# Expert loop of a fused perceiver, attention and mixture-of-experts layer on one core: one product, the output base and the next rows move, a scale changes engine

## The chip, the cores and the metric

The kernel runs on one core of one Trainium2 chip. The metric is the device time of one launch in microseconds; weights are laid out by the host beforehand and are not part of it. The core has TensorE (PE, matmuls and transposes into PSUM), VectorE (DVE), ScalarE (ACT), GpSimd (POOL) and SyncE (SP), which here only issues transfers. Each engine works through its own instructions in order and meets the others at semaphores.

## The reference, cut to what matters

The input is 128 entries of 32 rows of 512 numbers, in float32. Three residual blocks follow one another: a cross-attention block over a context of 257 rows for each entry, 16-head self-attention, and a feed-forward layer that has a shared expert and a routed part for some rows:

```python
sh = _ln(silu(x1) * x2, s_ln_g, s_ln_b)               # shared expert, every row
shared_out = einsum('bth,dh->btd', sh, sw3) + sb3
x_moe = x[index_b, index_t]                            # the chosen rows
expert_scores = sigmoid(x_moe @ eg_w.T + eg_b)
top1_idx = argmax(expert_scores + exp_bias, axis=-1)
weights = softmax([shared_score, top1_score])
z = _ln(silu(h1) * h2, sel_ln_g, sel_ln_b)             # 8 experts, H = 256
out_all = einsum('meh,edh->med', z, ew3) + eb3
final_out = shared_out.at[index_b, index_t].set(shared_out[chosen] * shared_w + expert_out * expert_w)
```

With the given indices every chosen row that exists lies in one tile of 128 rows, so the routed part is computed for that tile alone.

## The kernel before, in words

The 4096 rows are cut into 32 tiles of 128 rows (four entries). Tile 31 is the first one of the tensor, worked last, and is the one that holds the chosen rows. Three slots of buffers hold three tiles that are at different stages at once. `run_pipeline` (L167 on) works in rounds: in round n each engine walks a list of pairs (lag, unit) and does unit `name` of tile n - lag, if it has not been done. The order of an engine's instructions is the order of its list and nothing else. There are three tables of such lists, written out by a planner: FIRST for rounds 0 to 3, ORDER for rounds 4 to 29 and LAST from round 30 to the end. A unit is one step of a tile: `turn_h2` is four PE transposes (or the ACT or POOL work on them), `hidden` the product with W1 (or DVE's layer norm behind it), `project_k_l` the low half of a product whose operand is split into two float16 parts, and so on. Such a product is `high`/`high_t` (L1638, L1661), which needs ACT's float16 copy (L738), and `low`/`low_t` (L1647, L1673), which needs ACT's float32 copy (L746) and POOL's remainder (L631). A layer norm is DVE's moments (L1105 to L1107), POOL's power (L622), and DVE's scaling (L1111, L1114, L1118).

The routed part has 8 experts, whose weights for two halves of four (12 MB in all) are loaded into the arena during rounds 32 and 33, when the products of the earlier stages no longer need it (`e_first` to `e_sixth` on SP). Experts 0 to 3 are worked inside the rounds of LAST, as units of tile 31: `e_moments`, `e_norm`, `e_turn` (normalised rows and their transpose `e_xn_t`), `e_logits` and `e_gate_a/b/c` (choice and weight), then for each expert k `e_in{k}` (eight float32 matmuls, L1785), `e_bias{k}` (DVE, L1408), `e_gate{k}` (ACT tanh, L855), `e_z{k}` (DVE, `z_made`, L1359), `e_zn{k}` (`z_normed`, L1368: offset L1370, scale by the row's weight L1371), `e_zt{k}` (two transposes and ACT's copy) and `e_out{k}` (four matmuls, L1808). `e_total` adds them up in `o`.

Experts 4 to 7, and any further chosen tile, are worked in a hardware loop behind the pipeline; `redo` holds the number of passes, which is 1 for these inputs: one pass, for the second half of tile 31. The loop's body on each engine: PE (L1848 on) does the first two products at once (`expert_in(0)`, `expert_in(1)`, L1853), the transpose of the coefficients (L1861) and the bias product (L1864), then for each z two transposes (L1870), the product after next, and the four matmuls into `ps_v` (L1879). DVE (L1460 on) makes the coefficients (L1476 to L1482), then `biased(0)` (L1472), and for each k `z_made` (L1362 to L1366) and `z_normed` (L1370, L1371), and `biased(k+1)`. Between the moments of z 0 and its norm it makes the output's base (L1492 to L1494) and behind it L1499; behind z 2 it normalises the rows of the next pass (L1503, L1505). After the last product it adds `ps_v` to `o` (L1508), and works the gate of the next pass (L1338 to L1357), the last instructions of the program. ACT (L890 on) copies the coefficients (L892), does the gates (L885), starts the load of the next x2 (L896), copies each turned z (L900), and for the next pass L905, L907, L909. POOL does the five powers (L663), SP loads the next `old` rows (L564) and stores `o` (L587). The work for the next pass is done in the last pass too, where nobody uses it.

`ps_a`, `ps_t`, `ps_v` and `ps_e` are PSUM banks; `last_slot` in a row can be any of the buffers of slot 2, which share one tensor.

## Time and profile before, and how to read it

| | us |
|---|---|
| three runs, median | 1475.81 (1474.77 to 1477.35) |
| profiled execution, its own time | 1476.32 |
| its span | 1474.5 |
| PE busy | 1371.7 (93%) |
| DVE busy | 1133.4 (77%) |
| ACT busy | 586.0 (40%) |
| POOL busy | 523.8 (36%) |
| granted TensorE clock, mean | 0.987 |

The span runs from the first to the last instruction; the profiled execution's own time is 1.8 us longer. A timeline row gives start, duration, engine, line, operation, output and inputs, count, and in brackets how long the engine had been idle before it and what ended that. Line numbers are those of the kernel before. A row of windows gives each engine's busy time in a stretch. The clock of 1.00 is 2.4 GHz, 0.50 is 1.2 GHz.

### The profile page before, as it was taken

What the parts mean: (1) busy time and instruction counts of PE and PEld (TensorE: products, weight loads), DVE (VectorE), ACT (ScalarE), POOL (GpSimd) and SP (SyncE); (2) the same over time, 40 slices, a digit from 0 to 9 for tenths busy, and PEclk for the clock granted to TensorE, in tenths of its full rate; (3) what the DMA queues carried; (4) which work ended last, traced back from release to release, by engine and by line L of the source; (5) the groups of instructions that cost most, each with busy time, mean ns of one, the idle gap of its engine ahead of it and who ended that gap; (6) DMA issues with size and microseconds to landing.
All of it is one profiled execution on the core that took longest, in us unless ns stands there. A gap on an engine that the chain in (4) does not pass through costs nothing.

```text
span 1474.5 us, 32944 instructions
## 1 busy us (share of the span) xinstructions
PE 1371.7 (93%) x13724; PEld 858.8 (58%) x13725; DVE 1133.4 (77%) x2349; ACT 586.0 (40%) x1108; POOL 523.8 (36%) x534
## 2 busy tenths in 40 slices
PE   7679999999999999999999999999999999998976
PEld 3355566656656666665666666666666666565533
DVE  5776678777788777877778787787777878777865
ACT  2543344444444444443444444444434444343221
POOL 0133334433434333343443433334334433333310
PEclk9899999999999999999999999999999999999989
DMA  9622444333333444433333344443333324435240
GB/s 349 250 95 107 144 144 144 135 105 116 134 105 128 143 144 144 144 139 108 114 136 106 119 144 144 144 143 141 118 108 131 120 104 144 144 137 222 81 164 22
DMA packets 38659, 201.38 MB, mean 137 GB/s; under 512 B 5096, under 2 KB 5992, under 8 KB 28400
## 3 DMA queue, kind: packets, MB, share of 16 engines
q1 hardware_dynamic: 37648, 198.93, 37.6%
q8 instruction: 108, 1.77, 0.5%
q10 hardware_dynamic: 864, 0.36, 0.1%
q14 instruction: 39, 0.32, 0.1%
HBM read 182.24 MB, written 17.04 MB: 135 GB/s over the span
## 4 chain that ended last, share of the span: by engine, by line
PE 67%; DVE 18%; issue 5%; POOL 4%; ACT 4%; DMA 1%; SPq 0%; DVEq 0%; POOLq 0%; ACTq 0%
PE ps_a L1638 10%; PE ps_a L1661 8%; PE ps_t L1661 8%; PE ps_t L1625 6%; PE ps_a L1647 6%; PE ps_a L1702 4%; PE ps_a L1673 4%; PE ps_v L1638 4%; PE ps_t L1638 3%; POOL rstd L622 3%; DVE stats L1105 3%; DVE arena L1236 3%; PE ps_t L1694 2%; PE ps_t L1673 2%; PE ps_t L1745 2%
## 5 line engine op out<-in xcount | busy, mean ns | idle before, releaser
L631 POOL TENSOR_TENSOR act_l<-act_t,act_h 128x512 f16<-128x512 f32 (+1 forms) x176 | 199.0, 1131 | 385.1 <-ACT act_t L746 222.8
L622 POOL TENSOR_TENSOR rstd<-var,mhalf 128x1 f32<-128x1 f32 x224 | 185.4, 828 | 301.8 <-DVE var L1107 301.2
L631 POOL TENSOR_TENSOR last_slot<-last_slot 128x512 f16<-128x512 f32 x80 | 89.5, 1118 | 168.3 <-ACT last_slot L746 97.4
L738 ACT ACTIVATE act_h<-ps_t,scale 128x512 f16<-128x512 f32 (+1 forms) x110 | 70.8, 644 | 156.3 <-PE ps_t L1625 156.3
L1661 PE MATMUL ps_a<-act_h,arena 128*128 128x128 f16 x1408 | 87.4, 221 | 18.0 <-ACT act_h L738 18.0
L1661 PEld LDWEIGHTS ps_a<-act_h,arena 128*128 128x128 f16 x1408 | 81.7, 99 | 28.3 <-ACT act_h L738 22.4
L1661 PE MATMUL ps_t<-act_h,arena 128*128 128x128 f16 x1408 | 88.0, 222 | 4.5 <-ACT act_h L738 4.5
L1661 PEld LDWEIGHTS ps_t<-act_h,arena 128*128 128x128 f16 x1408 | 82.4, 99 | 6.3 <-issue 2.9
L1638 PE MATMUL ps_a<-arena,act_h 128*128 128x512 f16 x352 | 83.4, 380 | 1.6 <-ACT act_h L738 1.6
L746 ACT ACTIVATE act_t<-ps_t,scale 128x512 f32<-128x512 f32 (+1 forms) x110 | 70.3, 639 | 34.8 <-PE ps_t L1625 34.8
L1236 DVE TENSOR_SCALAR arena<-ps_a,unscale 32x512 f32<-32x512 f32 x64 | 48.2, 754 | 43.7 <-PE ps_a L1673 42.5
L1105 DVE BATCH_NORM_STATS2 stats<-rows 128x6 f32<-128x512 f32 x110 | 76.4, 695 | 3.8
L1625 PE MATMUL ps_t<-ident,rows 128*128 128x128 f32 x352 | 55.4, 280 | 14.0 <-DVE rows L1111 8.9
L1638 PE MATMUL ps_a<-w_parts,act_h 128*128 128x512 f16 x264 | 65.0, 383 | 1.3 <-ACT act_h L738 1.3
L1118 DVE SCALAR_TENSOR_TENSOR rows<-rows,rstd,beta 128x512 f32<-128x512 f32 x66 | 49.4, 748 | 21.5 <-POOL rstd L622 21.5
L1718 PE MATMUL ps_a<-arena,p_t 128*32 128x512 f32 x512 | 63.1, 611 | 1.5 <-ACT p_t L793 1.5
L1276 DVE STREAM_TRANSPOSE arena<-rows 32x512 f32<-32x512 f32 x88 | 61.8, 702 | 2.8
L1625 PEld LDWEIGHTS ps_t<-ident,rows 128*128 128x128 f32 x352 | 40.2, 141 | 36.1 <-DVE rows L1111 22.5
L738 ACT ACTIVATE last_slot<-ps_t,scale 128x512 f16<-128x512 f32 (+1 forms) x50 | 32.2, 644 | 62.8 <-PE ps_t L1625 62.8
L1638 PEld LDWEIGHTS ps_a<-arena,act_h 128*128 128x128 f16 x352 | 32.0, 98 | 41.9 <-ACT act_h L738 9.4
L1114 DVE SCALAR_TENSOR_TENSOR rows<-rows,mv,gamma 128x512 f32<-128x512 f32 x66 | 49.6, 751 | 0.0
L1702 PE MATMUL ps_a<-arena,q_t 128*32 128x257 f32 x704 | 44.3, 394 | 4.6 <-ACT q_t L783 4.6
(358 smaller groups left out, 3086.2 us busy)
## 6 DMA issues: line engine op xcount, KB each, us to landing
arena<-in_ctx_t SPq DMA_DIRECT2D x32, 2056.0 KB, 8.4
arena<-in_ctx_n SPq DMA_DIRECT2D x32, 2048.0 KB
ctx_last<-in_ctx_last SPq DMA_DIRECT2D x32, 256.0 KB
arena<-in_ew SPq DMA_DIRECT2D x8, 1024.0 KB, 6.1
x_in<-in_x SPq DMA_DIRECT2D x22, 256.0 KB, 7.2
x_scratch<-rows SPq DMA_DIRECT2D x22, 256.0 KB, 8.7
out<-rows SPq DMA_DIRECT2D x22, 256.0 KB, 2.0
arena<-in_ew SPq DMA_DIRECT2D x8, 512.0 KB, 7.3
```

Source lines behind the costliest of these rows:

```text
L622: nc.gpsimd.tensor_tensor(rstd[s][:], var[s][:], mhalf[:], ALU.pow).then_inc(rstd_ready[s], 1)
L631: nc.gpsimd.tensor_tensor(act_l[s][:, chunks], act_t[s][:, chunks], act_h[s][:, chunks], ALU.subtract).then_inc(act_l_ready[s], 1)
L738: nc.scalar.activation(act_h[s][:, 0:width // P].rearrange("p c r -> p (c r)"), bank[s][:, 0:width], ACT.Copy, scale=scale[:, k:k + 1]).th ...
L746: nc.scalar.activation(act_t[s][:, 0:width // P].rearrange("p c r -> p (c r)"), bank[s][:, 0:width], ACT.Copy, scale=scale[:, k:k + 1]).th ...
L1105: chain(nc.vector.bn_stats(stats[s][:], rows))
L1236: nc.vector.tensor_scalar(kbd[rows, :, :, h, :], ps_a[s][rows, :].rearrange("p (c g k) -> p c g k", c=C, g=G), unscale[rows, K_WATTN:K_WAT ...
L1625: mm = nc.tensor.transpose(out[s][:, c * P:(c + 1) * P], rows[s][:, lo + c * P:lo + (c + 1) * P], ident[:])
L1638: nc.tensor.matmul(bank[s][:], act_h[s][:, c, :], w[:, part, c, lo:lo + D], start=(c == 0 and part == 0), stop=False, skip_group_check=True)
L1647: mm = nc.tensor.matmul(bank[s][:], act_l[s][:, c, :], w[:, 0, c, lo:lo + D], start=False, stop=(c == chunks - 1), skip_group_check=True)
L1661: nc.tensor.matmul(bank[s][:, m * P:(m + 1) * P], w[:, part, c, lo + m * P:lo + (m + 1) * P], act_h[s][:, c, :], start=(m == 0 and c == 0 ...
L1673: mm = nc.tensor.matmul(bank[s][:, m * P:(m + 1) * P], w[:, 0, c, lo + m * P:lo + (m + 1) * P], act_l[s][:, c, :], start=False, stop=(c == ...
L1702: mm = nc.tensor.matmul(ps_a[s][T * g:T * (g + 1), 0:S], q_t[s][:, c, T * g:T * (g + 1)], ctx_t[:, c, g, :], start=(c == 0), stop=(c == C ...
```

## The change

Four edits to the loop, and new LAST lists for all four engines.

1. `expert_in(0)` of a pass is issued at the end of the pass before; for the first pass it is a new pipeline unit `e_in4` of tile 31 in round 34, ahead of `turn_z`. It waits for e_u_ready and for the last part of the expert weights.
2. DVE does `biased(0)` ahead of the coefficients, ACT `gated(0)` ahead of the copy of them. PE does the transpose of the coefficients behind `expert_in(1)`, then `expert_in(2)`, then the bias product; `expert_in(3)` stands behind the transposes of z 0.
3. The rows of the next pass and the output's base go behind the last z. The next x2 and `old` are loaded into buffers of their own at the start of the pass (`x2_next`, `old_next`) and ACT copies both into place at its end.
4. The scale of z by the row's weight goes from DVE (L1371) to ACT, as an activation in place behind DVE's offset; each gate goes ahead of the copy of the turned z. In the pipeline's `e_zn{k}` the scale stays on DVE.

In LAST, PE's list has in its second half (from `project_out` to `project_q`, for the tiles of rounds 30 and 31) the order of ORDER again, but `turn_xn`, `project_self` stand side by side, `project_v` and `head_scores` have changed places, and `head_mix` stands ahead of `turn_p` and `value_self_l`. For tile 31 `e_turn`, `e_logits`, `e_in0` go ahead of `turn_w`, `e_in1` behind `project_out`, `e_in3` behind `project_v_l`, `e_out1` and `e_zt2`, `e_out2` behind `project_out_l`, `e_zt3` behind `turn_x2n` and `e_out3` behind `ffn_in_l`.

```diff
 LAST = {
-    "pe": [(2, "project_k_l"), (3, "ffn_out"), (3, "ffn_out_l"), (1, "turn_pc"), (2, "project_q_l"), (2, "e_zt1"),
...
-        (1, "e_out0"), (0, "project_query_l"), (0, "context_scores"), (2, "ffn_in"), (2, "ffn_in_l"),
-        (1, "turn_x1n"), (1, "project_k"), (1, "project_q"), (2, "turn_z")],
+    "pe": [(3, "e_in4"), (3, "turn_z"), (2, "project_k_l"), (1, "turn_pc"), (2, "project_q_l"), (3, "ffn_out"),
+        (1, "context_mix"), (3, "ffn_out_l"), (2, "project_v"), (2, "head_scores"), (2, "project_v_l"),
+        (1, "e_turn"), (0, "turn_xn"), (1, "e_logits"), (0, "project_self"), (1, "e_in0"), (2, "e_out1"),
+        (2, "e_zt2"), (0, "project_self_l"), (0, "value_self"), (1, "turn_w"), (0, "self_scores"),
+        (1, "context_out"), (1, "context_out_l"), (2, "e_in3"), (2, "head_mix"), (0, "turn_p"), (0, "value_self_l"),
+        (0, "self_mix"), (2, "project_out"), (1, "e_in1"), (1, "turn_h2"), (2, "project_out_l"), (1, "hidden"),
+        (1, "hidden_l"), (2, "e_out2"), (1, "e_zt0"), (1, "e_in2"), (0, "turn_h"), (2, "turn_x2n"), (2, "e_zt3"),
+        (0, "project_query"), (0, "project_query_l"), (2, "ffn_in"), (1, "e_out0"), (0, "context_scores"),
+        (2, "ffn_in_l"), (1, "turn_x1n"), (1, "project_k"), (2, "e_out3"), (1, "project_q"), (1, "e_zt1")],
...
 # SP, in the loop
-                    sp.wait_ge(e_x2_used, i + 1)
+                    sp.wait_ge(x2_copied, i + 1)
                     sp.sem_inc(stats_seen, 1)
                     load_old(i + 1)
+                    sp.wait_ge(e_old_loaded, 16 * i + 32)
...
 # ACT, in the loop
+                    gated(i, 0)
                     act.wait_ge(coef_turned, i + 1)
                     nc.scalar.copy(coef_t[:], ps_gate[0:NE, P:2 * P]).then_inc(coef_t_ready, 1)
-                    gated(i, 0)
...
                     for k in range(EH):
+                        act.wait_ge(z_normed, EH * i + k + 1)
+                        nc.scalar.activation(z, z, ACT.Copy, scale=mine_coef[:, k:k + 1]).then_inc(e_z_ready, 1)
+                        if k + 1 < EH:
+                            gated(i, k + 1)
                         act.wait_ge(e_z_turned, EH * (i + 1) + k + 1)
                         nc.scalar.copy(z_t.rearrange("p c r -> p (c r)"), ps_t[s_b][:, 0:H]).then_inc(e_z_t_ready, 1)
...
+                    act.wait_ge(xn_turned, i + 2)
+                    nc.scalar.copy(flat_rows(e_xn_t), ps_t[s_last][:]).then_inc(xn_t_ready, 1)
+                    act.wait_ge(e_x2_used, i + 1)
+                    nc.scalar.copy(x2[:], x2_next[:])
+                    act.wait_ge(e_old_loaded, 16 * i + 32)
+                    nc.scalar.copy(old[:], old_next[:]).then_inc(x2_copied, 1)
...
 # DVE, in the loop
+                    biased(0)
                     step(nc.vector.tensor_copy(now[:], flags[:, bass.ds(half * 2, 2)]))
...
-                    biased(0)
                     for k in range(EH):
                         dve.wait_ge(e_z_turned, EH * (i + 1) + k)
                         z_made(step, EH * (i + 1), k)
-                        if k == 0:
...
-                        z_normed(step, (1 + EH) * (i + 1) + k + 1 + (k > NEXT_ROWS), mine_coef[:, k:k + 1])
+                        dve.wait_ge(e_rstd_ready, (1 + EH) * (i + 1) + k + 1)
+                        nc.vector.scalar_tensor_tensor(z, z, e_rstd[:], sel_b, ALU.mult, ALU.add).then_inc(z_normed, 1)
                         if k + 1 < EH:
                             biased(k + 1)
...
+                    dve.wait_ge(e_x2_loaded, 16 * i + 32)
+                    expert_moments(step, x2_next[:])
+                    dve.wait_ge(e_rstd_ready, (1 + EH) * (i + 1) + EH + 1)
+                    nc.vector.tensor_scalar(e_xn[:], x2_next[:], e_mv[:, 0:1], e_rstd[:], ALU.subtract, ALU.mult
+                                            ).then_inc(xn_ready, 1)
+                    dve.wait_ge(x2_copied, i + 1)
+                    dve.sem_inc(stats_seen, 1)
+                    dve.wait_ge(e_out_stored, 16 * i + 16)
+                    step(nc.vector.tensor_scalar(o, o, now[:, 1:2], None, ALU.mult))
+                    step(nc.vector.scalar_tensor_tensor(o, old[:], now[:, 0:1], o, ALU.mult, ALU.add))
+                    step(nc.vector.tensor_tensor(old[:], old[:], x2[:], ALU.subtract))
+                    step(nc.vector.scalar_tensor_tensor(o, old[:], one[:, 7:8], o, ALU.mult, ALU.add))
+                    dve.sem_inc(e_x2_used, 1)
...
 # PE: the new unit, and the loop
+                def e_in_next(s, r, tile):
+                    if tile == FINAL:
+                        pe.wait_ge(e_u_ready, EH)
+                        pe.wait_ge(part_loaded[3], PART_COUNTS[3])
+                        for c in range(C):
+                            mm = nc.tensor.matmul(ps_a[s_a][:], e_xn_t[:, c, :],
+                                                  of_arena(HALF + EW12[0] + c * 2 * H, 2 * H), start=(c == 0),
+                                                  stop=(c == C - 1))
+                        mm.then_inc(e_u_done, 1)
...
-                    expert_in(0)
-                    expert_in(1)
+                    expert_in(1, half)
                     pe.wait_ge(coef_ready, i + 1)
                     nc.tensor.transpose(ps_gate[0:NE, P:2 * P], pick[:, 3, :], ident[:]).then_inc(coef_turned, 1)
+                    pe.wait_ge(e_u_ready, EH * (i + 1) + 1)
+                    expert_in(2, half)
                     pe.wait_ge(coef_t_ready, i + 1)
...
-                        if k + 2 < EH:
-                            pe.wait_ge(e_u_ready, EH * (i + 1) + k + 1)
-                            expert_in(k + 2)
-                        if k == EH - 1:
-                            gate_logits(i + 2)
+                        if k == 0:
+                            pe.wait_ge(e_u_ready, EH * (i + 1) + 2)
+                            expert_in(3, half)
...
+                    turn_expert_rows(ps_t[s_last], i + 2)
+                    gate_logits(i + 2)
+                    expert_in(0, half_next)
```

## Rows read from the trace of the kernel before

**Rows 1.** Windows by stage: a round of ORDER, rounds 30, 32, 33, the loop

```profile
core 0: us, PE busy (x) PEld busy (x) DVE busy (x) ACT busy (x) POOL busy (x), PEclk, DMA share, GB/s
1221.75:1262.60 40.85, 39.67 (x425) 25.45 (x423) 32.06 (x67) 16.96 (x34) 15.92 (x16) 1.00 0.36 128
1262.60:1305.90 43.30, 39.94 (x425) 25.63 (x422) 34.15 (x67) 16.92 (x33) 15.64 (x16) 1.00 0.37 135
...
1349.20:1398.10 48.90, 42.94 (x321) 24.10 (x319) 38.01 (x87) 14.80 (x30) 13.79 (x15) 0.97 0.45 164
1398.10:1434.00 35.90, 26.81 (x165) 12.06 (x162) 24.71 (x49) 9.07 (x18) 7.60 (x9) 0.92 0.43 162
1434.00:1474.50 40.50, 28.77 (x71) 12.93 (x71) 22.43 (x64) 4.01 (x12) 3.25 (x5) 0.88 0.08 26
```

**Rows 2.** Timeline of PE in round 30: its two longest waits

```profile
1288.58 1.90 PE L1638 MATMUL ps_a<-arena,last_slot 128*128 128x512 f16 x8 [0.78 <-ACT last_slot L738]
...
1296.07 1.94 PE L1702 MATMUL ps_a<-arena,q_t 128*32 128x257 f32 x32 [0.78 <-ACT q_t L783]
```

**Rows 3.** Timeline of tile 31 in round 33, up to the loop

```profile
1417.79 0.75 DVE L1282 SCALAR_TENSOR_TENSOR rows<-ps_a,unscale,rows 128x512 f32<-128x512 f32 x1 [0.30 <-PE ps_a L1647]
...
1420.34 0.55 DVE L1111 TENSOR_SCALAR rows<-rows,mv,rstd 128x512 f32<-128x512 f32 x1 [0.67 <-POOL rstd L622]
...
1425.33 0.75 DVE L1293 SCALAR_TENSOR_TENSOR rows<-ps_a,unscale,b 128x512 f32<-128x512 f32 x1 [4.44 <-PE ps_a L1647]
...
1429.39 0.69 PE L1625 MATMUL ps_t<-ident,v_n 128*128 128x128 f32 x2 [4.10 <-DVE v_n L1118]
...
1433.49 0.75 DVE L1316 SCALAR_TENSOR_TENSOR rows<-ps_a,unscale,b 128x512 f32<-128x512 f32 x1 [2.05 <-PE ps_a L1647]
```

**Rows 4.** Timeline of rounds 32 and 33: durations used in the sum

```profile
1356.54 0.72 ACT L757 ACTIVATE v_n<-v_n,row_scale 128x512 f32<-128x512 f32 x1 [0.42 <-DVE row_scale L1186]
...
1397.01 0.39 PE L1625 MATMUL ps_t<-ident,v_n 128*128 128x128 f32 x2
...
1399.90 0.75 DVE L1316 SCALAR_TENSOR_TENSOR rows<-ps_a,unscale,b 128x512 f32<-128x512 f32 x1
...
1402.43 3.70 PE L1785 MATMUL ps_a<-arena,last_slot 128*128 128x512 f32 x8
...
1418.44 1.98 PE L1808 MATMUL ps_t<-arena,p_t 128*128 128x512 f32 x4 [0.46 <-ACT p_t L862]
```

**Rows 5.** Windows of PE ahead of the loop: busy, granted clock, DMA

```profile
1424.00:1428.00 4.00, 1.29 (x6) 1.00 0.01 3
1428.00:1432.00 4.00, 2.05 (x6) 0.56 0.00 0
```

**Rows 6.** Timeline of the loop's first part on VectorE

```profile
1436.23 0.17 DVE L1476 COPY now<-flags 128x2 f32 x1 [1.27 <-issue]
...
1440.17 0.69 DVE L1472 TENSOR_TENSOR last_slot<-ps_a,arena 128x512 f32<-128x512 f32 x1 [2.79 <-PE ps_a L1853]
...
1447.62 0.69 DVE L1494 TENSOR_TENSOR last_slot<-last_slot 128x512 f32<-128x512 f32 x1
```

**Rows 7.** Timeline of the loop from z 1 to z 2

```profile
1452.78 0.43 DVE L1364 SCALAR_TENSOR_TENSOR p_n<-last_slot 128x256 f32<-128x256 f32 x1 [1.53 <-ACT last_slot L885]
...
1455.02 0.48 DVE L1370 SCALAR_TENSOR_TENSOR p_n<-p_n,rstd,ctx_last 128x256 f32<-128x256 f32 x1 [0.44 <-POOL rstd L663]
...
1455.54 0.35 DVE L1371 TENSOR_SCALAR p_n<-p_n,mine_coef 128x256 f32<-128x256 f32 x1
...
1456.68 0.42 DVE L1362 SCALAR_TENSOR_TENSOR last_slot<-last_slot 128x256 f32<-128x256 f32 x1 [0.18 <-PE ps_t L1870]
...
1456.95 0.42 ACT L885 ACTIVATE last_slot<-last_slot 128x256 f32<-128x256 f32 x1
```

**Rows 8.** Timeline of the loop's end on VectorE

```profile
1470.06 0.69 DVE L1508 TENSOR_TENSOR last_slot<-ps_v,last_slot 128x512 f32<-128x512 f32 x1 [3.15 <-PE ps_v L1879]
...
1473.88 0.16 DVE L1357 TENSOR_TENSOR one<-one,sel 128x1 f32<-128x1 f32 x1
```

More of the change, by code:

```diff
@@ L127 @@
 LAST = {
-    "pe": [(2, "project_k_l"), (3, "ffn_out"), (3, "ffn_out_l"), (1, "turn_pc"), (2, "project_q_l"), (2, "e_zt1"),
-        (1, "context_mix"), (2, "head_scores"), (2, "e_in3"), (0, "turn_xn"), (2, "project_v"), (2, "project_v_l"),
-        (1, "turn_w"), (2, "e_out1"), (0, "project_self"), (1, "e_turn"), (0, "project_self_l"), (1, "e_logits"),
-        (0, "value_self"), (1, "e_in0"), (0, "self_scores"), (2, "e_zt2"), (1, "context_out"), (1, "context_out_l"),
-        (0, "value_self_l"), (0, "turn_p"), (2, "head_mix"), (1, "e_in1"), (0, "self_mix"), (2, "e_out2"),
-        (2, "project_out"), (2, "project_out_l"), (1, "e_zt0"), (2, "e_zt3"), (2, "e_out3"), (1, "turn_h2"),
-        (1, "hidden"), (0, "turn_h"), (1, "hidden_l"), (1, "e_in2"), (0, "project_query"), (2, "turn_x2n"),
-        (1, "e_out0"), (0, "project_query_l"), (0, "context_scores"), (2, "ffn_in"), (2, "ffn_in_l"),
-        (1, "turn_x1n"), (1, "project_k"), (1, "project_q"), (2, "turn_z")],
@@ L156 @@
+    "pool": [(3, "turn_z"), (0, "xn_moments"), (0, "turn_xn"), (1, "e_norm"), (2, "e_zn2"), (2, "head_scores"),
+        (1, "turn_w"), (1, "context_out"), (2, "head_mix"), (1, "e_zn0"), (0, "self_mix"), (2, "e_zn3"),
+        (1, "turn_h2"), (2, "project_out"), (0, "turn_h"), (1, "hidden"), (2, "turn_x2n"), (1, "out_norm"),
+        (1, "e_zn1"), (1, "turn_x1n"), (2, "silu")],
 }
@@ L563, in load_old @@
                 def load_old(i):
[L564 removed]
+                    sp.dma_start(old_next[:], a["out"][bass.ds(tile_of(sp, i), 1)].rearrange("a p d -> (a p) d")
                                  ).then_inc(e_old_loaded, 16)
@@ L1839, in _ @@
                     **{f"e_in{k}": e_in(k) for k in range(EH)}, **{f"e_zt{k}": e_zt(k) for k in range(EH)},
-                    **{f"e_out{k}": e_out(k) for k in range(EH)}})
+                    **{f"e_out{k}": e_out(k) for k in range(EH)}, "e_in4": e_in_next})
                 pe.wait_ge(out_ready[s_b], r_b + 1)
```

83 lines of the change are left out of this document (29 added, 54 removed).

## The prediction

> **What bounds the kernel now.** I read the windows by stage first. In a round of ORDER, PE is busy 39.67 of 40.85 us; rounds 30 and 31 (one stands for both) do the same tile work in 43.30 with 39.94 busy, so their surplus is waiting [rows 1]. Round 32 is PE with gaps (42.94 of 48.90), round 33 and the loop are not PE's: 26.81 of 35.90 and 28.77 of 40.50 us [rows 1]. There the timeline shows a chain through DVE, with PE, ACT and POOL taking single steps between. Only what comes after 1262.6, some 212 us, can change: the tables of the rounds before 30 are untouched.
>
> In the loop DVE starts at 1436.23, and its first real work, the bias of product 0, comes at 1440.17 after 2.79 us of waiting for PE [rows 6], which started eight half-rate matmuls only when the pipeline was over. Then the first z waits for a gate that stands on ACT behind the coefficients, the base is made while z 0 is due, the gate of each z stands behind the copy of the z before, and the next rows stand between z 2 and z 3. The output is added at 1470.06 and the last instruction ends at 1474.04 [rows 8]. So the loop takes DVE 1474.04 - 1436.23 = 37.81 us, for four z whose steps are about 4 us each.
>
> **The loop after the change**, with DVE's first instruction at 0. `biased(0)` runs 0 to 0.7, as its product is long done. Five small steps of about 0.2 [rows 6] and the wait for them end at 1.9; ACT's gate 0 is made meanwhile. A z goes as in rows 7: L1362 0.45, from L1364 to L1370 1455.02 - 1452.78 = 2.24 (moments and POOL's power in it), so L1370 starts 2.7 after L1362: at 4.6. It takes 0.48, then the scale on ACT. That operation is not in the trace in this size: below, DVE's own 0.35; above, the same operation at twice the width, 0.72 [rows 4]; I take 0.45, by the gate's 0.42 at the same width [rows 7], plus a hop of 0.05. z 0 is ready at 5.6.
>
> PE: product 1 stands ahead of DVE's start and ends about 1.4; transpose of the coefficients to 1.7; product 2 takes 3.5 (3.70 with its drain [rows 4]) to 5.2; the bias product about 1.0 (half of 1.98 [rows 4]) to 6.1. So z 0's transposes start at 6.1, 0.5 late, and end at 6.5. Product 3 fills PE to 10.0 and four matmuls of z 0 (1.7) to 11.7. z 1: L1362 at 6.5, ready at 10.2, turned only at 12.1, 1.5 late behind PE. From there PE is no longer in the way: z 2 ready at 15.8, turned 16.3; z 3 ready at 20.0, turned 20.4, copied by ACT to 20.8, multiplied to 22.8. What each cycle sheds is the gate: it ended at 1457.37 with L1362 already over at 1457.10 [rows 7], and now it is ahead of the copy. The biases (0.69 each) lie between L1370 and the turned z.
>
> DVE after z 3's L1370 (19.5): the next rows, 0.7 moments, small steps, power, 0.55 norm, 2.4 together, to 21.9; the base, four steps of 0.5 to 0.75 with L1494's 0.69 among them [rows 6], 2.9 together, to 24.8. So the moved work is half covered by PE's last 3.3 us (19.5 to 22.8), and 2.0 of it is now on the path: **what is late next is DVE itself**. L1508 at 24.8. Behind it L1508 to the end takes 1474.04 - 1470.06 = 3.98 [rows 8], plus 0.5, since ACT copies x2 and `old` (two of about 0.6, from 24.8) ahead of the tanh. End at 29.3. PE's extra product for nobody ends at about 28.3, under that. The loop loses 37.8 - 29.3 = **8.5 us**.
>
> The queues that work is moved past: SP issues the load of `old` at the start and waits for it there, 20 us before the store is due; ACT issues the x2 load at about 2, ahead of a wait at 5; POOL does the same five powers in order. Both transfers go into buffers that nobody reads before 19.5. I cost them at nothing; without that cover each would be a transfer of some 4 us on the path.
>
> **The end of round 33.** X is the end of tile 31's L1111, 1420.89; from it to turn_z is 8.50 (1429.39) [rows 3]. PE idled 4.10 us ahead of turn_z; into that gap now go `e_out3` and `e_in4`. But `e_zt3`'s copy stands on ACT behind the gate of `ffn_in`, which waits for DVE's L1293 (X + 4.44 to 5.19 [rows 3]): the copy ends at X + 6.0. Then four matmuls (1.7) and eight (3.5): turn_z at X + 11.2, not 8.5. That is **+2.7**. On the other side PE does not cool. With the idle 4.1 us the granted clock fell to 0.56 in the window 1428 to 1432, half rate [rows 5], and from turn_z to L1316 it took 1433.49 - 1429.39 = 4.10 [rows 3], where tile 30 at full clock took 1399.90 - 1397.01 = 2.89 [rows 4]: **-1.2**. The new gap is 1.6 us (X + 4.4 to X + 6.0), against the 4.10 behind which it fell. `e_in4` waits for the weights of the second half: from 1424 on the DMA share is 0.01 [rows 5], so they have landed, 4 us ahead of its start. The nearest end if the clock falls all the same: up to 7 of the 12 matmuls at 0.43 more, +3.0.
>
> **Rounds 30 and 31.** The second half of PE's list is ORDER's again: the waits of 0.78 ahead of `hidden` and of `context_scores` [rows 2] get a filler each. In its first half `turn_xn` and `project_self`, and `value_self_l` and `self_mix`, now stand next to each other, each pair with an ACT or DVE step between that nothing covers, 0.7 to 0.8 each. I followed one round step by step with the durations of rows of rounds 29 to 31 and came out 0.5 shorter; two rounds, **-1.0**. Bounds: ORDER's length, 43.30 - 40.85 = -2.45 each [rows 1]; above, the covers gone and none gained, +1.0 each.
>
> **Rounds 32 and 33 up to L1282 of tile 31** (1417.79 [rows 3]). `turn_w` of tile 31 goes behind `e_in0` (+0.4); ACT's half copies first and `project_out_l` as filler, `hidden_l` up to 1.0 earlier; the head of tile 31 about 0.9 later, since `e_z1` now stands ahead of L1293 of tile 30 and `e_in3` ahead of `head_mix`; `project_out` 0.9 earlier, as `e_out2` no longer stands ahead of it. Net **+0.15**, bounds -2 and +2.
>
> **Sum**: -8.5 + 2.7 - 1.2 - 1.0 + 0.15 = -7.85. Against the profiled execution's own 1476.32 (its span of 1474.5 and 1.8 around it) that is 1468.5. The median of the runs, 1475.81, is 0.5 lower, so the forecast is **1468.0**.
>
> The scale's move is the one edit that a rule speaks against. The row above: DVE does it in 0.35, ACT's nearest in 0.42 [rows 7]; by that each z is ready 0.1 later, 0.3 in all as z 0 and z 1 wait for PE anyway, and DVE's 0.35 saved lies in its wait for the turned z. It pays only where the bias then fits in. The Trainium skill, "ScalarE: Activation LUTs", section "Rules for kernel authors", says to put a plain multiplication on VectorE and not on ScalarE, up to about three times faster there in bf16. Taken at that for float32 the sum would be some 2 us worse; the two rows, 0.35 and 0.42, speak for the small figure.
>
> **Rivals.**
> A. The tables go all the way: rounds 30 and 31 take ORDER's 40.85, -4.9 in place of -1.0: 1464. For it: the second half is the same list. Against: the two uncovered pairs. 0.14.
> B. The tail pays: PE's clock falls ahead of `e_out3` (+3.0), or ACT and PE, now closer to each other, lose that in rounds 32 and 33: 1471.5. For it: the clock is below full in round 32 as well as in 33, 0.97 and 0.92 [rows 1]. Against: the new gap is far shorter. 0.17.
> C. The gain is given back nearly whole: the loop's end in sequence (base behind PE's last sum, +2), B's +3.0, and the upper bounds of rounds 30 and 31 (+3.0 over -1.0), so -7.85 + 8.0: within 0.2% of before, 1476. 0.07.
> D. Slower: `head_mix`. In each of rounds 30, 31 and 33 the head products stand behind `project_v` (1.7 later, eight matmuls in 1.90 with drain [rows 2]) and `head_mix` ahead of `value_self_l` and `turn_p` (1.1 earlier), in round 33 behind `e_in3` (3.5). If DVE's chain through L1276 was just in time, PE's whole queue stands: up to 2.8 in each of three rounds and 3.5 once, +11.9 for the tables in place of -0.85, so +4.9 in all: 1481. It decides from the point at which L1276's last transpose ends later than PE's `context_out_l`; by my walk it is 0.4 earlier in round 30. 0.05.
>
> **Chances.** Forecast 0.57 (1465.5 to 1470.5), A 0.14, B 0.17, C 0.07, D 0.05. A measurement of this kernel can tell about 0.2%, 2.95 us, from no change. Faster by more: 0.57 + 0.14 + 0.17 = 0.88; within: 0.07; slower: 0.05. The range takes in A and B: 1463.5 to 1472.5; outside lie C, D and the ends of A.
>
> **What would show it.** In the loop: L1472 first on DVE and without a wait; L1362 to L1362 of the next z about 5.6, 4.2, 4.2; L1331 on `x2_next` and the base behind the fourth L1370; L1508 at +24.8 of DVE's first instruction; ACT's scale 0.42 to 0.5. In round 33: PE with no gap over 2 us ahead of turn_z and 1.00 as granted clock through to the loop, turn_z about 11.2 behind L1111. Rounds 30 and 31 at 42.3 to 43.3 each. Wrong would be: a loop of over 32 us, the turned z waiting for PE at z 2 and z 3, L1282 of tile 31 not at 1416 to 1418, or `e_in4` waiting for a transfer.

## The result and the profile after

The changed kernel takes 1479.91 us (median of 20 runs, 1477.17 to 1481.95) against 1476.42 for the kernel before (20 runs beside it): a ratio of 1.0023, 95% interval 1.0016 to 1.0029. It is slower by 3.5 us, where 8 less was forecast, and it lies outside the range. The profiled execution spans 1479.1 us against 1474.5, so 4.6 more; the account below is of that one. With 1481.63 us it was 1.7 above the median, so it is one of the longer executions.

Windows by stage of the kernel after (the edges moved with the work, so that each holds the same units as in [rows 1]); the second and third are rounds 30 and 31:

```profile
core 0: us, PE busy (x) PEld busy (x) DVE busy (x) ACT busy (x) POOL busy (x), PEclk, DMA share, GB/s
1221.75:1262.60 40.85, 39.67 (x425) 25.42 (x423) 32.30 (x67) 16.51 (x32) 15.94 (x16) 1.00 0.37 129
1262.60:1306.30 43.70, 40.50 (x424) 25.02 (x422) 32.24 (x67) 16.91 (x34) 15.92 (x16) 1.00 0.34 121
1306.30:1350.00 43.70, 40.50 (x425) 25.04 (x423) 32.25 (x67) 16.93 (x33) 15.93 (x16) 1.00 0.37 137
1350.00:1403.40 53.40, 45.32 (x310) 24.17 (x308) 37.64 (x87) 14.69 (x30) 13.45 (x15) 0.94 0.43 156
1403.40:1442.70 39.30, 30.96 (x182) 14.05 (x179) 25.02 (x49) 9.40 (x19) 7.60 (x9) 0.96 0.40 148
1442.70:1479.10 36.40, 30.23 (x71) 12.45 (x71) 20.92 (x60) 7.37 (x18) 3.43 (x5) 0.86 0.09 29
```

The loop is shorter, 36.40 in place of 40.50, but by half of what was forecast; every stage from round 30 up to it is longer, round 32 most (53.40 for 48.90).

Timeline of PE in round 32 after:

```profile
1362.07 0.63 PE L1760 MATMUL ps_t<-ident,last_slot 128*128 128x128 f32 x4 [2.78 <-DVE last_slot L1388]
1363.52 1.81 PE L1766 MATMUL ps_e<-mask_self,last_slot 128*128 128x9 f32 x8 [0.82 <-ACT last_slot L841]
1365.18 6.26 PE L1791 MATMUL ps_a<-arena,last_slot 128*128 128x512 f32 x8
1371.28 0.60 PE L1631 MATMUL ps_t<-ident,v_n 128*128 128x128 f32 x4
1372.56 1.90 PE L1644 MATMUL ps_a<-arena,act_h 128*128 128x512 f16 x8 [0.68 <-ACT act_h L763]
...
1380.39 3.67 PE L1791 MATMUL ps_a<-arena,last_slot 128*128 128x512 f32 x8 [1.29 <-DVE last_slot L1413]
```

These are `e_turn`, `e_logits`, `e_in0`, `turn_w` of tile 31, its `context_out`, and `e_in1`. `e_in0` takes 6.26 where it takes 3.7 at full clock (it was below full clock before as well, with 5.32); `turn_w` and a wait of 0.68 for its copy now follow it, so all of tile 31 stands behind those 6.26 us; and `e_in1` waits 1.29 for `e_bias0`, with `hidden` of tile 31 queued behind.

Timeline of round 33 after, PE and DVE:

```profile
1414.41 0.44 PE L1814 MATMUL ps_e<-ident,p_n 128*128 128x128 f32 x2 [2.54 <-DVE p_n L1430]
1414.69 5.29 PE L1791 MATMUL ps_a<-arena,last_slot 128*128 128x512 f32 x8
1419.91 1.08 PE L1751 MATMUL ps_t<-arena,v_n 128*32 128x128 f32 x32
...
1427.38 0.55 DVE L1120 TENSOR_SCALAR rows<-rows,mv,rstd 128x512 f32<-128x512 f32 x1 [0.66 <-POOL rstd L624]
...
1433.89 1.98 PE L1824 MATMUL ps_t<-arena,p_t 128*128 128x512 f32 x4 [1.55 <-ACT p_t L864]
1435.71 3.60 PE L1802 MATMUL ps_a<-arena,last_slot 128*128 128x512 f32 x8
1439.14 0.38 PE L1631 MATMUL ps_t<-ident,v_n 128*128 128x128 f32 x2
```

`e_zt2` waits 2.54, and behind that wait `e_in3` takes 5.29 at half clock. From the end of L1120 (1427.93, the X of the prediction) to turn_z at 1439.14 is 11.21: the forecast 11.2. The step that answers to L1282 in [rows 3] is now L1291; it starts at 1424.83, 7.04 late.

The loop after, PE and DVE:

```profile
1444.29 5.39 PE L1869 MATMUL ps_a<-arena,last_slot 128*128 x8 [2.42 <-issue]
1454.21 0.44 PE L1885 MATMUL ps_t<-ident,p_n 128*128 128x128 f32 x2
1459.64 0.38 PE L1885 MATMUL ps_t<-ident,p_n 128*128 128x128 f32 x2
1463.84 0.44 PE L1885 MATMUL ps_t<-ident,p_n 128*128 128x128 f32 x2 [1.29 <-ACT p_n L904]
1468.10 0.69 PE L1885 MATMUL ps_t<-ident,p_n 128*128 128x128 f32 x2 [0.59 <-ACT p_n L904]
1469.34 3.68 PE L1892 MATMUL ps_v<-arena,p_t 128*128 x4 [0.55 <-ACT p_t L908]
```

```profile
1444.83 0.69 DVE L1479 TENSOR_TENSOR last_slot<-ps_a,arena 128x512 f32<-128x512 f32 x1 [1.38 <-issue]
...
1473.06 0.69 DVE L1514 TENSOR_TENSOR last_slot<-ps_v,last_slot 128x512 f32<-128x512 f32 x1 [0.52 <-PE ps_v L1892]
...
1478.44 0.16 DVE L1366 TENSOR_TENSOR one<-one,sel 128x1 f32<-128x1 f32 x1
```

PE enters 2.42 us late with no producer named: "issue". Its queue is loading registers then, one from `redo` at 1441.6 and two from `halves` at 1442.7 and 1443.5, as the views of the two tables show (duration in ns, first and last start):

```profile
L412 PEldq TENSOR_LOAD <-redo x1: 494/494/494, 1441.6 to 1441.6; - x1
...
L418 PEldq TENSOR_LOAD <-halves x2: 311/312/312, 1442.7 to 1443.5; - x2
```

Product 1 takes 5.39 for 3.7, the last sum 3.68 for 1.98. The clock of PE there (windows: PE busy, granted clock, DMA share, GB/s):

```profile
1442.00:1444.00 2.00, 0.00 (x0) 1.00 0.00 0
1444.00:1446.00 2.00, 1.71 (x4) 0.87 0.34 131
1446.00:1448.00 2.00, 2.00 (x4) 0.50 0.00 0
...
1466.00:1468.00 2.00, 1.51 (x2) 0.50 0.00 0
1468.00:1470.00 2.00, 1.35 (x3) 0.50 0.00 0
1470.00:1472.00 2.00, 2.00 (x3) 0.50 0.00 0
```

From DVE's first instruction to the end the loop is now 1478.60 - 1444.83 = 33.77, against 37.81 before: 4.04 gained of the 8.5.

### The profile page after: what moved, and what is told of

Same layout as the page of the kernel before. It is cut to its first block, busy times and chain, and to the rows that moved or that the text cites. A ratio compares the mean times of both kernels' runs of the same rounds, so it can differ in the third digit from the quotient of the medians.

```text
span 1479.1 us, 32967 instructions
## 1 busy us (share of the span) xinstructions
PE 1380.9 (93%) x13732; PEld 859.2 (58%) x13733; DVE 1128.3 (76%) x2345; ACT 589.1 (40%) x1114; POOL 524.5 (35%) x534
## 4 chain that ended last, share of the span: by engine, by line
PE 69%; DVE 17%; ACT 4%; issue 4%; POOL 4%; DMA 1%; SPq 0%; DVEq 0%; POOLq 0%; ACTq 0%
PE ps_a L1644 11%; PE ps_a L1667 8%; PE ps_t L1667 8%; PE ps_t L1631 6%; PE ps_a L1653 6%; PE ps_a L1708 4%; PE ps_a L1679 4%; PE ps_t L1644 3%; PE ps_v L1644 3%; POOL rstd L624 3%; DVE stats L1114 3%; DVE arena L1245 3%; PE ps_t L1679 2%; PE ps_t L1700 2%; PE ps_t L1751 2%
## 5 line engine op out<-in xcount | busy, mean ns | idle before, releaser
L1679 PE MATMUL ps_t<-act_l,arena 128*128 128x128 f16 x704 | 47.6, 221 | 0.0
```

The costliest lines, as they stand in the source:

```text
L1679: mm = nc.tensor.matmul(bank[s][:, m * P:(m + 1) * P], w[:, 0, c, lo + m * P:lo + (m + 1) * P], act_l[s][:, c, :], start=False, stop=(c == ...
```

## The experiments

To compare profiles I cut the end of each trace at five marks: the start of `project_k` (its ps_a product) of tiles 28, 30 and 31, L1282 of tile 31 (L1291 in the kernel after), and turn_z's transposes in the last round; "end" is the end of the last DVE instruction. All stages in us, each from one profiled execution; `e_in0` is its duration, as a reading of the clock in round 32.

| kernel | median | ratio to before, 95% | rounds 30, 31 | round 32 (e_in0) | to L1282 | to turn_z | to the end |
|---|---|---|---|---|---|---|---|
| before | | | 86.68 | 48.16 (5.32) | 24.37 | 11.60 | 44.65 |
| after | 1479.91 | 1.0023 (1.0016 to 1.0029) | 87.45 | 52.75 (6.26) | 26.07 | 14.31 | 39.46 |
| loop_only | 1469.46 | 0.9956 (0.9943 to 0.9969) | 86.66 | 48.17 (5.31) | 24.36 | 11.58 | 37.84 |
| tables_only | 1483.54 | 1.0044 (1.0031 to 1.0056) | 87.44 | 52.71 (6.18) | 26.06 | 11.60 | 45.84 |
| regs_early | 1475.94 | 0.9999 (0.9990 to 1.0008) | 87.43 | 52.27 (5.28) | 24.35 | 15.69 | 34.47 |
| loop_regs | 1466.15 | 0.9934 (0.9921 to 0.9947) | 86.67 | 49.84 (6.69) | 24.35 | 11.60 | 35.66 |
| fill10 | 1465.93 | 0.9933 (0.9919 to 0.9946) | 86.67 | 48.14 (3.68) | 24.36 | 11.60 | 34.53 |
| after_fill | 1472.72 | 0.9975 (0.9966 to 0.9984) | 87.45 | 49.26 (3.68) | 24.40 | 15.84 | 36.15 |

After less before, stage by stage: 0.77 + 4.59 + 1.70 + 2.71 - 5.19 = 4.58, the 4.6 of the two spans.

**Which half loses: loop_only and tables_only.** The first is the loop of after in the tables of before, the second the reverse.

```diff
 # loop_only: LAST of before, and in "pe"
-(1, "project_k"), (1, "project_q"), (2, "turn_z")],
+(1, "project_k"), (1, "project_q"), (2, "e_in4"), (2, "turn_z")],
 # tables_only: the kernel before with LAST of after, less (3, "e_in4")
```

> The loop of after with the tables of before, and e_in4 put just ahead of turn_z in PE's list. Theory (the tables lose about 7 us up to L1282 of tile 31, the loop itself gains 4, and the warm end of round 33 gains 1.2): L1282 of tile 31 at 1417.8 as before, turn_z within 0.5 of before, clock 1.00 from turn_z to the loop; the loop 33.8 us on DVE as in after. So 4 to 5 us under before: about 1471.5. Rival (the loss sits in the loop or in how it is entered, and the tables only showed it): no gain over before, 1475 to 1478.

> The tables of after (without e_in4), the loop of before. Theory: L1282 of tile 31 at 1424 to 1425, 6 to 7 us later than before, and the loop at 37 to 38.5 as before, so 1482 to 1484. Rival (the tables are worth about nothing, as predicted, and the loop is what lost): 1475 to 1477.

The theory held in both, 1469.46 and 1483.54, the first 2 us better than expected. The loop is a gain by itself, the tables a loss. In loop_only turn_z stood 11.58 behind L1282, so `e_in4` in PE's gap costs nothing. In tables_only, where `e_out3` waits 1.55 for its copy just as in after but no `e_in4` follows, it stood 11.60 behind, so that wait costs nothing by itself either. The 2.7 comes of the two together: `e_in4`, which needs no copy, is queued behind the `e_out3` that waits for one.

The loop of tables_only also shows the register loads, without the change to the loop: PE enters it 1.59 late behind "issue", with two loads at 1439.8 and 1440.8, where before it was 0.60.

**How PE enters the loop: regs_early and loop_regs.** One in the tables of after, one in those of before.

```diff
 def e_in_next(s, r, tile):
     if tile == FINAL:
+        passes.append(passes_to_do(pe))
...
-                count = passes_to_do(pe)
+                count = passes[0]
...
-                    half, half_next = half_of(pe, i), half_of(pe, i + 1)
+                    half = half_of(pe, i)
...
-                    expert_in(0, half_next)
+                    expert_in(0, half_of(pe, i + 1))
```

> After, with PE's load of the pass count made at e_in4 in round 33, and the load of the next half moved to just ahead of the last product of the pass. Theory (PE enters the loop late because of three register loads that nothing covers): product 1 starts 1.5 to 2 us earlier (gap of 2.42 down to about 1), the first z's transposes 1.5 to 2 us earlier, and if the clock stays up, product 1 at 3.7 in place of 5.4. So 1.5 to 3.5 us under after. Rival (PE is not what the first z waits for, or the late end of the loop eats it): within 0.5 of after.

> The run with the loop of after in the tables of before, and in it PE's pass count loaded at e_in4 and the next half's load put ahead of the last product. Theory: the gap ahead of product 1 falls from 2.43 to 0.60 as it did with the tables of after, product 1 takes 3.69 in place of 5.39, so the first z's transposes come 3.5 earlier, of which DVE's own chain takes back nothing at the end: 3 to 3.5 us under that run's 1469.5, so 1466 to 1466.5, and over 0.6% faster than before. Rival (the end of the loop is DVE's, and a part of PE's late start lay in the shade of the first z): 0 to 1.5 us under it.

Both gained over their own base, 4.0 and 3.3 us in the medians (the intervals of loop_regs and loop_only overlap by 0.0004; in their traces the loop is 29.92 against 32.08). The timeline of loop_regs at the loop, PE and then DVE:

```profile
1433.73 3.70 PE L1872 MATMUL ps_a<-arena,last_slot 128*128 x8 [0.60 <-issue]
1442.29 0.44 PE L1888 MATMUL ps_t<-ident,p_n 128*128 128x128 f32 x2
1447.71 0.38 PE L1888 MATMUL ps_t<-ident,p_n 128*128 128x128 f32 x2
1451.92 0.44 PE L1888 MATMUL ps_t<-ident,p_n 128*128 128x128 f32 x2 [1.29 <-ACT p_n L904]
1456.17 0.44 PE L1888 MATMUL ps_t<-ident,p_n 128*128 128x128 f32 x2 [1.29 <-ACT p_n L904]
1457.16 2.85 PE L1895 MATMUL ps_v<-arena,p_t 128*128 x4 [0.55 <-ACT p_t L908]
```

```profile
1436.08 0.69 DVE L1479 TENSOR_TENSOR last_slot<-ps_a,arena 128x512 f32<-128x512 f32 x1 [1.38 <-issue]
...
1460.83 0.69 DVE L1514 TENSOR_TENSOR last_slot<-ps_v,last_slot 128x512 f32<-128x512 f32 x1 [0.23 <-DVE last_slot L1511]
```

The wait behind "issue" is 0.60, product 1 takes 3.70, z 0 is turned at +6.21 (forecast 6.1), z 1 to z 3 at +11.6, +15.8, +20.1 (12.1, 16.3, 20.4), and the output is added at +24.75, where 24.8 was forecast. The loop is 29.92 long (forecast 29.3).

regs_early shows something else. Its `e_in3` happened to run at full clock (3.60), and L1282 came 1.72 earlier than in after; but then the half clock fell in `ffn_in`, 3.43 for 1.90:

```profile
1427.11 3.43 PE L1644 MATMUL ps_a<-w_parts,act_h 128*128 128x512 f16 x8 [0.22 <-ACT act_h L740]
```

So turn_z was 1.38 later behind L1282, and of the 1.72 only 0.34 was left. The two columns have to be read together.

**The scale's move: loop_regs_dve.** loop_regs with the multiplication by the coefficient on DVE.

```diff
-nc.vector.scalar_tensor_tensor(z, z, e_rstd[:], sel_b, ALU.mult, ALU.add).then_inc(z_normed, 1)
+step(nc.vector.scalar_tensor_tensor(z, z, e_rstd[:], sel_b, ALU.mult, ALU.add))
+nc.vector.tensor_scalar(z, z, mine_coef[:, k:k + 1], None, ALU.mult).then_inc(e_z_ready, 1)
```

> As the run with the loop of after, the tables of before and early register loads, but each z is multiplied by its coefficient on DVE as before, not on ScalarE. Theory (ScalarE's copy takes 0.51 and a hop, DVE's 0.35 with no hop, and the bias fits in either way): same to 1 us faster, as z 2 and z 3 lie on the path and each is ready 0.2 to 0.35 earlier. Rival (DVE is the bound and its 0.35 for each z counts): 0.7 to 1.4 us slower.

1468.97, ratio 0.9946 (0.9933 to 0.9959), which overlaps with loop_regs' 0.9921 to 0.9947: the times lean to ScalarE without deciding. What I had expected, the same or up to 1 us faster on DVE, did not come; the sign is the rival's. The traces say more. In loop_regs_dve:

```profile
1452.00 0.44 PE L1887 MATMUL ps_t<-ident,p_n 128*128 128x128 f32 x2 [1.14 <-DVE p_n L1496]
...
1453.01 0.42 DVE L1369 SCALAR_TENSOR_TENSOR last_slot<-last_slot 128x256 f32<-128x256 f32 x1 [0.46 <-DVE last_slot L1477]
...
1456.63 0.44 PE L1887 MATMUL ps_t<-ident,p_n 128*128 128x128 f32 x2 [1.26 <-DVE p_n L1496]
```

Here z 3's first step waits for its own bias, no longer for PE: the cycle is 4.63 against 4.25, and the loop 30.48 against 29.92. ScalarE does the operation in 0.51 against 0.35, and still wins: what counts is whose queue it leaves. The Trainium skill, "ScalarE: Activation LUTs", section "Rules for kernel authors", would have it on VectorE; the durations agree in direction (by a factor of 1.5), the loop's length does not.

**Fillers for the clock.** They are 128x128 float32 products of the identity into a free part of ps_e, for nobody. The Trainium skill, "TensorE: Matmul & The Clock Gate", section "HAM oscillation — how this bites in real kernels", describes a like pattern, where each stage of matmuls starts cold because PE waited for a DMA ahead of it. The trace of after agrees as far as it goes, but here the wait is one for DVE: `e_turn` waits 2.78, the granted clock is 0.89 from 1362 to 1364 and 0.50 from there to 1370, and `e_logits` and `e_in0` run in that.

```diff
+def filler(n):
+    for _ in range(n):
+        nc.tensor.matmul(ps_e[:, 2 * P:3 * P], ident[:], ident[:], start=True, stop=True,
+                         skip_group_check=True)
...
+                        filler(a)
                         turn_expert_rows(ps_t[s_a], 1)
+                        filler(b)
```

> After, with small matmuls for nobody (128 columns, into a free part of ps_e): 8 ahead of the loop, 8 ahead of product 1, 8 behind each of the sums of z 1 and z 2. Theory (PE's half clock in product 1 and in the last sums costs about 3 us): granted clock 1.00 from 1442 to the end, L1892 of z 3 at 2.0 in place of 3.7, the last product 3.7 or less, 1.5 to 3 us under after. Rival (the fillers stand on the path, or the clock is down in places where DVE sets the end): within 1 us of after, or over it.

> After with the early register loads, and small matmuls for nobody in PE's waits of rounds 32 and 33: 20 ahead of e_turn, 6 behind it, 20 ahead of e_zt2. Theory (half clock costs 1.7 us in e_logits and e_in0 and 1.7 in e_in3, more than before): granted clock 1.00 from 1362 to 1420, e_in0 3.7 in place of 6.3, e_in3 3.7 in place of 5.3, L1291 of tile 31 3 to 4 us earlier than in after; 1472 to 1473. Rival (the clock falls where PE is not the bound, DVE's chain sets head_mix): under 1.5 us off regs_early.

> The loop of after in the tables of before with early register loads, and small matmuls for nobody: 20 ahead of e_turn and 6 behind it in round 32, 8 behind each of the sums of z 1 and z 2 in the loop. Theory: e_in0 3.7 in place of 5.3 or more, the last sum of the loop 2.0 in place of 2.9, each on the chain: 1.5 to 3.5 us under the run without them, 1463 to 1464.5. Rival (round 32's chain is DVE's and the last sum lies beside DVE's base): 1465.5 to 1466.5.

> The loop of after in the tables of before with early register loads, and 8 small matmuls for nobody behind each of the sums of z 1 and z 2, none in round 32. Theory (the fillers ahead of e_turn cost what they gave, those in the loop are free and keep the last sum at full clock): 0.5 to 1.5 us under the run without any, 1465 to 1465.7. Rival (the last sum at half clock lies beside DVE's base and nothing is gained): 1466 to 1467.

warm_loop: 1478.75 (1.0016, 1.0008 to 1.0025), 1.2 under after, at the edge between theory and rival: clock 1.00 to the end, but its fillers ahead of product 1 held PE up by as much as they gave. warm_rounds: 1475.47 (0.9992, 0.9982 to 1.0001), no better than regs_early's 1475.94, as its rival had it. best_warm: 1468.03 (0.9941, 0.9928 to 0.9955), not under loop_regs: a miss. The reason is in best_warm's trace:

```profile
1358.47 4.63 PE L1759 MATMUL ps_e<-ident 128*128 128x128 f32 x40
1362.93 0.60 PE L1765 MATMUL ps_t<-ident,last_slot 128*128 128x128 f32 x4
```

20 fillers are 40 records and take 4.63 us, in a wait of 2.8: I had taken half of that, and they stood on the chain (round 32 was 49.58, though `e_in0` took 3.68). The 20 ahead of `e_zt2` in warm_rounds took 4.63 as well, in a wait of 2.54. In loop_regs_z, without those, the last sum was 1.98 and the loop 29.14 in place of 29.92, as forecast, but its median, 1467.35 (0.9938, 0.9924 to 0.9951), lies above both ranges and can't be told from loop_regs'. So two more, with fillers that fit:

> The loop of after in the tables of before with early register loads, and small matmuls for nobody that fit into PE's waits: 10 ahead of e_turn (2.3 us by the 4.63 that 20 took, in a wait of 2.77), 2 behind it, 5 behind each of the sums of z 1 and z 2. Theory (round 32's half clock is on the chain: the kernels with e_in0 at 6.7 had 49.84 us from project_k to project_k, those at 5.3 had 48.17): e_in0 3.7, 46.6 to 47 us from project_k to project_k; last sum 2.0; 1463 to 1464.5. Rival (DVE, and not PE, sets round 32 once e_in0 is short: e_in1 waits for e_bias0): 48 us or more, 1465 to 1467.

> After with early register loads and small matmuls that fit: 10 ahead of e_turn, 2 behind it, 8 (1.9 us) in the wait of 2.54 ahead of e_zt2. Theory: e_in0 3.7 and e_in3 3.6, from project_k to project_k 50.5 to 51, from there to L1291 24.35; 1474 to 1475. What it is then over the kernel with the tables of before and the same fillers is the lists' own cost without the clock: 0.8 in rounds 30 and 31, 3.5 to 4 in round 32, 2.7 ahead of turn_z. Rival (half clock costs nothing in these tables): 1475.5 to 1477.

fill10 gave the loop 28.78 and the last stage 34.53, but in round 32 the rival was right: 48.14 with `e_in0` at 3.68, the same as before with it at 5.32. In PE's timeline `head_mix` and `e_in1` of tile 31's round now wait for DVE, 0.75 and 0.57:

```profile
1371.47 1.08 PE L1751 MATMUL ps_t<-arena,v_n 128*32 128x128 f32 x32 [0.75 <-DVE arena L1285]
1373.12 3.67 PE L1798 MATMUL ps_a<-arena,last_slot 128*128 128x512 f32 x8 [0.57 <-DVE last_slot L1413]
```

after_fill, 1472.72, did better than expected: round 32 fell from 52.27 to 49.26. So the half clock is worth 3.0 to 3.5 us in round 32 with the tables of after (52.27 and 52.75 with `e_in0` at 5.28 and 6.26, less 49.26), and nothing to 1.7 with those of before (48.16 and 49.84 with it at 5.32 and 6.69, less 48.14). At full clock the new order costs 49.26 - 48.14 = 1.12 there, and nothing from there to L1282 (24.40 and 24.36). Behind L1282 after_fill loses again: `e_in3` ran at full clock, but `ffn_in` took 3.11, and turn_z came 15.84 behind L1282, as in regs_early. From `project_k` to turn_z that makes 40.24 us, against 40.38 in after. With these tables no trace has full clock all the way to turn_z, and what that would give stays open.

**Undoing single moves.** All on regs_early (1475.94). The moves, in LAST:

```diff
 # fix_zt2, "pe": (2, "e_zt2") behind (2, "head_mix"), just ahead of (2, "project_out")
 # fix_both: and (1, "turn_w") ahead of (1, "e_in0")
 # order_r32: "pe": (1, "turn_w") ahead of (1, "e_in0"); "dve": (1, "e_gate_c"), (1, "e_bias0") ahead of (1, "context_out")
 # order_r32_r33: and "pe": (2, "head_scores"), (2, "e_in3") ahead of (2, "project_v")
 # ctx_first: "dve": (1, "context_scaled") ahead of (1, "e_moments"); "act": it, turn_xn, turn_w, turn_w_t ahead of (1, "e_turn");
 #            "pe": (0, "turn_xn"), (1, "turn_w") ahead of (1, "e_turn")
 # ctx_first_bias: and "dve": (1, "e_gate_c"), (1, "e_bias0") ahead of (1, "context_out")
```

> After with the early register loads, and e_zt2 put behind head_mix, ahead of project_out, in PE's list. Theory (in round 33 e_zt2 waits 2.54 us for DVE's e_zn2, with e_in3 and head_mix queued behind it, and the clock falls on that idle time): e_in3 starts at 1411.9 and takes 3.7, head_mix starts about 3.5 to 4 us earlier, L1291 of tile 31 2 to 4 us earlier than in regs_early; the time 2 to 4 us under regs_early, 1472 to 1474. Rival (head_mix is late because its own input on DVE is): within 0.7 us of regs_early.

> As the run with e_zt2 behind head_mix, and turn_w put ahead of e_in0 in PE's list as well. Theory (tile 31's turn_w stands 6.26 us behind e_in0, and its whole context_out, hidden and project_k with it): context_out of tile 31 3 to 5 us earlier, project_k 2 to 4 us earlier, head_scores likewise; another 2 to 4 us off, in all 1468.5 to 1471.5. Rival (the rest of round 32 is bound by e_in1 on e_bias0 and by PE's sum of work, and gives the gain back): under 1 us off the run with e_zt2 alone.

> After with the early register loads, turn_w put ahead of e_in0 on PE, and e_gate_c and e_bias0 put ahead of context_out on DVE, as they stood before. Theory (round 32 loses 1.3 us to turn_w behind e_in0 and 1.3 to e_in1 waiting for e_bias0): no wait of 1.29 ahead of e_in1, hidden of tile 31 about 2.5 us earlier than in regs_early at the same clock, L1291 of tile 31 likewise; 1473 to 1474. Rival (the chain takes it back behind e_in1, where hidden waits for its own input): within 1 us of regs_early.

> As the run before it, with head_scores and e_in3 put ahead of project_v on PE as well, as they stood before. Theory (head_scores stands 1.9 us behind project_v and DVE's chain from it to head_mix is 8.3 us whatever stands on PE): head_mix 1.5 to 2 us earlier and L1291 too, 1471.5 to 1472.5; rounds 30 and 31 also gain up to 1 each if their heads were late. What is left over the run with the tables of before is then the 2.7 of e_out3 and e_in4 and 1 to 2 of rounds 30 and 31. Rival (head_mix is held by something else on DVE): no gain over the run before it.

> After with the early register loads, and tile 31's context chain ahead of the expert rows again on three engines: context_scaled ahead of e_moments on DVE, context_scaled, turn_w and turn_w_t ahead of e_turn on ACT, turn_xn and turn_w ahead of e_turn on PE. Theory (in round 32 context_scaled stands on ACT behind e_turn's copy and e_scores, 9 us later than before, and PE's turn_w can't run in the gap ahead of e_turn): context_scaled on ACT at about 1357, turn_w in PE's gap ahead of e_turn, nothing between e_in0 and context_out; from project_k of tile 30 to that of tile 31 1.3 to 2 us less than in regs_early's 52.27 at the same e_in0; the time 1474 to 1475, if rounds 30 and 31 do not lose by it. Rival (the context chain isn't the one that sets project_k of tile 31, or rounds 30 and 31 pay): within 0.5 of regs_early's 1475.9, or over.

> As the run before it, with e_gate_c and e_bias0 ahead of context_out on DVE too. Theory: no wait for e_bias0 ahead of e_in1, another 1.3 to 1.6 us, so that project_k to project_k is 49 to 50 against the 48.2 to 49.8 of the kernels with the tables of before, and the time 1472.5 to 1473.5; what then remains over the run with the tables of before (1466.2) is the 2.7 of e_out3 and e_in4 and the 1 us of rounds 30 and 31, plus half clock where it falls on the chain. Rival (another wait takes its place): project_k to project_k over 51.

| kernel | median | rounds 30, 31 | round 32 (e_in0) | to L1282 |
|---|---|---|---|---|
| fix_zt2 | 1477.15 | 87.42 | 52.78 (6.21) | 27.59 |
| fix_both | 1477.54 | 87.86 | 52.23 (5.98) | 27.70 |
| order_r32 | 1474.90 | 87.87 | 52.02 (6.00) | 25.88 |
| order_r32_r33 | 1479.52 | 87.87 | 50.43 (4.55) | 31.03 |
| ctx_first | 1480.30 | 92.87 | 50.49 (5.38) | 26.08 |
| ctx_first_bias | 1478.35 | 92.84 | 50.58 (5.38) | 26.21 |

None of my six moves reached its forecast. fix_zt2 put `e_in3` into the wait, but `head_mix` then waited 2.84 for DVE's L1287: it had not been late because of what stands ahead of it on PE. There and in fix_both the half clock then fell in `project_out` (3.32 and 3.60 for 1.90), a part of why "to L1282" is over 3 us longer than in regs_early. order_r32 did free `e_in1` (`hidden` 11.12 behind `context_out`, against 12.72 in regs_early), but `turn_w` in its new place waits 1.11 for ACT's v_n and `e_in0` starts that much later. order_r32_r33 was the worst of the misses. Its heads were scored early, and yet:

```profile
1412.22 0.69 ACT L818 ACTIVATE v_n<-ps_v,unscale 128x512 f32<-128x512 f32 x1 [7.48 <-PE ps_v L1655]
1412.81 0.62 ACT L823 ACTIVATE rows<-rows 128x512 f32<-128x512 f32 x1
...
1419.23 1.93 PE L1753 MATMUL ps_t<-arena,v_n 128*32 128x128 f32 x32 [3.30 <-DVE arena L1287]
```

ACT's list still had `project_v`'s copy ahead of the heads' exponentials, so they waited 3.5 us for the very product that I had put behind. ctx_first shows the same from the other side. In the trace of after ACT does L759 (`context_scaled` of tile 31) at 1365.69, where it was at 1356.54 [rows 4], because its list has `e_turn` and `e_scores` ahead. Put back on three engines, it gave round 32 the forecast 1.8 us (52.27 to 50.49), and took 5.4 in rounds 30 and 31, which run the same lists. ctx_first_bias freed `e_in1` of its wait as expected (1.16 in ctx_first, none here), but `e_in2` then waited 1.38 for DVE's L1415, and round 32 was no shorter.

## Why the prediction was wrong

The profiled executions differ by +4.58 where the sum said -7.85. Of these 12.4 us, 6.1 lie in rounds 32 and 33 up to L1282, 4.5 in the loop and 1.8 in rounds 30 and 31. Two steps of the prediction failed at their mechanism: the overlap at the loop's start, and the term +0.15 for rounds 32 and 33, in which `turn_w` behind a product of 3.7 or 6.3 us was counted as 0.4.

**The loop's walk was right, its start was not.** "Product 1 stands ahead of DVE's start and ends about 1.4" is the step that failed here: the transpose behind it started 4.7 after DVE's first instruction (1449.52 against 1444.83). I had counted matmuls and DMAs in PE's queue and not the register loads. Before, there were two, and the first was issued under half-rate matmuls of the round's end; the change adds one (`half_next`) and, by making that end fast, uncovers all three. That is 3.2 of the missing 4.5 us (z 0 turned at +9.38 against +6.21 in loop_regs), the wait (2.42 against 0.60) and the clock in product 1 (5.39 against 3.70) in about equal parts. The rest is half clock in the last sums: the loop is 28.78 long in fill10, and as long in regs_early, where the last sum took 1.98 without any filler. With the loads mended the walk's numbers came out within about 0.6 us at every point.

**The end of round 33.** +2.7 was +2.71, by the mechanism that I gave: four matmuls and then eight behind one copy. "PE does not cool", -1.2, was -1.26 (turn_z to DVE's L1325: 2.84 against 4.10 in [rows 3]). But PE then stood idle for 2.42 us behind it and the clock fell one step later, in product 1: what was won ahead of the loop was lost in it. Rival B had the right thing at the wrong place.

**Rounds 30 and 31**, -1.0 forecast, are +0.77, and 87.42 to 87.46 in all the traces with these tables unchanged up to there, against 86.66 to 86.69 in those with the tables of before. My walk of one round has the wrong sign. The uncovered pair is there, `self_mix` waiting 0.87 in each round (timeline of after):

```profile
1285.21 1.10 PE L1700 MATMUL ps_t<-v_n,p_t 128*128 128x512 f32 x2 [0.87 <-ACT v_n L771]
```

Both covers did give back their 0.78: in the rows of after neither `hidden` (1289.25 and 1332.97) nor `context_scores` (1298.16 and 1341.88) waits. Against them stand this 0.87, and 0.31 and 0.78 ahead of `turn_xn` and `project_self`. So PE waits a little less in such a round than before, but it is busy 0.54 longer with as many matmuls (one round from `project_k` to `project_k`, PE busy, granted clock, DMA share and GB/s, before and then after):

```profile
1301.92:1345.26 43.34, 39.98 (x421) 1.00 0.35 128
...
1302.29:1346.01 43.72, 40.52 (x421) 1.00 0.37 135
```

Why the same matmuls take PE longer in the new order no run shows.

**Rounds 32 and 33 up to L1282**, +0.15 with bounds of 2, are +6.29, the largest error. I had `turn_w` behind `e_in0` at +0.4; it is a place behind a product that takes 3.7 or 6.3, and I did not ask what a falling clock does to the unit that I saw moved behind it. By the runs: 1.1 us are the order itself, 3.5 half clock in `e_logits` and `e_in0`, 1.7 half clock in `e_in3` (and where `e_in3` was spared, some 1.4 of that came back in `ffn_in`). "The clock is below full in round 32 as well" stood in my text as a word for rival B, but B's +3.0 was the price of half clock in `e_out3` and `e_in4`; for round 32 I had no price.

**Rival D** gave 1481, near the truth, by a mechanism that the traces do not show, so that is luck. From `project_k` of tile 31 to L1282 is 24.35 to 24.40 us with either tables when the clock is up, and in rounds 30 and 31 `head_mix` waits for nothing: it costs nothing where it stands. It was given 0.05, rightly for its mechanism; what was missing is a rival in which the chain of tile 31 comes to run through a half-rate `e_in0`.

The other points held: `e_in4` waited for no transfer, ACT's scale was 0.51 (0.42 to 0.5 expected), still a gain in the loop's length (29.92 against 30.48), the loads past which work was moved were never waited for in the loop.

A version that beats both kernels is the loop of after with the tables of before, `e_in4` ahead of turn_z, and early register loads: 1466.15, and 1465.93 with fillers; the two can't be told apart.
